# First-batch context first, two weight transfers instead of four, and a layer 1 that opens on the rounded half of its input

## The reference, cut to what matters

```python
# x: (8, 256, 256)   ctx: (8, 120, 256)   w1, w2: (1024, 256)   h1, h2: (1024, 1024)   w3: (256, 1024)
n = layernorm(x)
x = x + (gelu_tanh(n @ ctx.T) * (n @ ctx.T)) @ ctx       # per batch, the "attention" part
n = layernorm(x)
h = silu(n @ w1.T * s1) * (n @ w2.T * s2)                # layer 1
h = gelu(h @ h1.T * sh1)                                 # the two square layers
h = gelu(h @ h2.T * sh2)
x = x + h @ w3.T * s3                                    # layer 4
```

## Time and profile before

| | us |
|---|---|
| median of 3 runs | 334.35 |
| lowest, highest | 331.96, 334.93 |
| the profiled execution, its own time | 334.1 |
| its span in the profile | 332.3 |
| PE busy | 324.5 (98%) |
| DVE busy | 264.6 (80%) |
| ACT busy | 218.1 (66%) |
| POOL busy | 47.3 (14%) |

### The profile page before, as it was taken

The page is one execution under the profiler, slowest core; times in us unless marked ns, Lnnn a source line. Parts: engine busy times, 40 slices in busy tenths (PEclk is TensorE's granted clock), DMA queues, the critical chain, the costliest instruction groups (busy, mean ns, idle before and its releaser), DMA issues.

```text
span 332.3 us, 4771 instructions
## 1 busy us (share of the span) xinstructions
PE 324.5 (98%) x1643; PEld 274.4 (83%) x1643; DVE 264.6 (80%) x492; ACT 218.1 (66%) x367; POOL 47.3 (14%) x86
## 2 busy tenths in 40 slices
PE   7999999999999999999999999999999999999994
PEld 4699888888878888888998888888887888888994
DVE  3577888796996999998579666398899798987594
ACT  2355838648596886778914564977679687785840
POOL 6247020201100022112130003000100000110000
PEclk9999999999999999999999999999999999999999
DMA  7769999949657762735306033345575863443003
GB/s 227 257 208 292 207 225 368 407 172 306 192 176 250 284 240 90 228 129 155 100 0 231 24 126 126 128 127 189 189 225 197 278 249 130 126 131 123 0 32 104
DMA packets 23213, 60.22 MB, mean 181 GB/s; under 512 B 1680, under 2 KB 7184, under 8 KB 20880
## 3 DMA queue, kind: packets, MB, share of 16 engines
q0 software_dynamic: 13728, 37.75, 38.0%
q1 hardware_dynamic: 9168, 21.60, 19.0%
q10 hardware_dynamic: 288, 0.51, 0.5%
HBM read 49.36 MB, written 6.29 MB: 167 GB/s over the span
## 4 chain that ended last, share of the span: by engine, by line
PE 95%; DVE 1%; DMA 1%; POOL 1%; issue 0%; ACT 0%; DVEq 0%
PE P L1290 61%; PE P L1242 18%; PE P L1319 9%; PE P L1214 2%; PE P L1198 2%; PE P L1206 2%; DMA xs<-in_x 1%; POOL rs L434 1%; PE P L1391 1%; PE P L1384 1%; PE P L1398 0%; PE P L1329 0%; DVE xn L819 0%; POOL rs L432 0%; DVE xs L831 0%
## 5 line engine op out<-in xcount | busy, mean ns | idle before, releaser
L1290 PE MATMUL P<-TR,WR 128*128 128x512 f32 x896 | 205.5, 390 | 0.0
L1290 PEld LDWEIGHTS P<-TR,WR 128*128 128x128 f32 x896 | 167.7, 188 | 35.4 <-DVE H L915 0.8
L591 ACT ACTIVATE TR<-H 128x512 fp32r<-128x512 f32 x112 | 68.1, 626 | 29.1 <-DVE H L894 26.4
L899 DVE TENSOR_TENSOR TR<-H,TR 128x512 fp32r<-128x512 f32 x112 | 73.8, 686 | 7.6 <-ACT TR L591 5.9
L1242 PE MATMUL P<-X,W 128*128 128x512 f32 (+1 forms) x320 | 62.7, 351 | 0.1
L1242 PEld LDWEIGHTS P<-X,W 128*128 128x128 f32 x320 | 51.7, 189 | 8.1 <-DVE X L836 0.5
L894 DVE TENSOR_TENSOR H<-H 128x512 f32<-128x512 f32 x64 | 42.0, 684 | 0.0
L872 DVE SCALAR_TENSOR_TENSOR H<-P,sc,SLY 128x512 f32<-128x512 f32 (+1 forms) x40 | 25.2, 639 | 19.1 <-ACT SLY L581 10.0
L581 ACT ACTIVATE SLY<-P,sc 128x512 f32<-128x512 f32 (+1 forms) x40 | 23.7, 601 | 18.6 <-PE P L1242 18.4
L605 ACT ACTIVATE H<-P 128x512 f32<-128x512 f32 x48 | 27.8, 593 | 11.6 <-PE P L1290 11.6
L625 ACT ACTIVATE H<-H,sc 128x512 f32<-128x512 f32 x40 | 27.4, 713 | 10.7 <-DVE H L915 10.7
(11 more groups left out here) (72 smaller groups left out, 197.9 us busy)
## 6 DMA issues: line engine op xcount, KB each, us to landing
WR<-blocks_h POOLq DMA_DIRECT2D x16, 1024.0 KB, 5.1
WR<-in_h POOLq DMA_DIRECT2D x12, 1024.0 KB, 5.2
H<-in_h POOLq DMA_DIRECT2D x8, 512.0 KB, 12.0
blocks_h<-H SPq DMA_DIRECT2D x4, 1024.0 KB, 6.6
SLY<-in_h SPq DMA_DIRECT2D x8, 512.0 KB, 4.5
SLY<-in_w SPq DMA_DIRECT2D x6, 512.0 KB, 4.6
W<-in_w POOLq DMA_DIRECT2D x4, 512.0 KB, 7.8
WR<-in_w POOLq DMA_DIRECT2D x2, 1024.0 KB, 5.1
```

The lines of the kernel that those rows point to most:

```text
L591: eng.activation(TR[:, f % RING, 0, :], operand(c, L, s, kk), ACT.Copy).then_inc(s_hi, 1)
L899: eng.tensor_tensor(TR[:, f % RING, 1, :], operand(c, L, s, kk), TR[:, f % RING, 0, :].bitcast(f32), ALU.subtract).then_inc(s_lo, 1)
L1290: out_ = eng.matmul(bank(c, L, s, m)[:, :], WR[r % WRING][:, at:at + 128], TR[:, f % RING, h, :], start=(s in FRESH[L] and kk == 0 and h = ...
```

## The change

In the beginning of the program:

- The context arrays lie in memory with the batch ahead of the feature half, so that one batch's part is one transfer. ACT no longer issues them. SP issues, in this order: the two halves of `x` of batch 0, context of batch 0 (two transfers, with semaphores `e_cf` and `e_ct`), `x` of batch 1, context of batch 1 (two transfers), the scales.
- POOL issues `W12` in two transfers (w1, then w2) instead of four, after waiting for `s_tab`, which ACT signals when its first table load is done.
- On PE `score(1)` no longer stands ahead of layer 1. The first half of layer 1 waits for `s_X0` and runs the rounded parts of groups 0 and 1 (two matmuls each), waits for `s_X1`, runs their other parts, then `score(1)`, then groups 2 to 15. `weigh(1)` follows group 5 instead of group 3.
- `score(2)` moves from between the two halves to behind group 1 of the second half.
- The filler counts become 16, 3, 3, 2, 16, 3 instead of 16, 2, 2, 1, 14, 2.

```diff
-SPIN = (16, 2, 2, 1, 14, 2)
+SPIN = (16, 3, 3, 2, 16, 3)
...
# SP
             for j in range(2):
                 eng.dma_start(xs[:, j, :], x_v[0, :, j, :]).then_inc(s_x0[j], 16)
+            eng.dma_start(cf[:, 0, 0, :, :], ctx_feat[:, 0, 0, :, :]).then_inc(e_cf, 16)
+            eng.dma_start(ct[:, 0, 0, :], ctx_tok[:, 0, :]).then_inc(e_ct, 16)
             load_x(1)
+            eng.dma_start(cf[:, 0, 1, :, :], ctx_feat[:, 0, 1, :, :]).then_inc(s_cf[0], 16)
+            eng.dma_start(ct[:, 0, 1, :], ctx_tok[:, 1, :]).then_inc(s_ct[0], 16)
             eng.dma_start(sc[:, :], cols).then_inc(s_sc, 16)
-            for i in range(4):
+            for i in range(2):
                 eng.wait_ge(s_w12[i], 16)
...
# POOL
             def load_w12(i):
-                eng.dma_start(W12[:, i % 2, i // 2, :], w12[i % 2][:, i // 2, :]).then_inc(s_w12[i], 16)
+                eng.dma_start(W12[:, i, :, :], w12[i]).then_inc(s_w12[i], 16)
...
-            for i in range(4):
+            eng.wait_ge(s_tab, 1)
+            for i in range(2):
                 load_w12(i)
...
# ACT
             table(ACT.Gelu_apprx_tanh)
-            eng.dma_start(cf[:, 0, :, :, :], ctx_feat[:, 0, :, :, :]).then_inc(s_cf[0], 16)
-            eng.dma_start(ct[:, 0, :, :], ctx_tok[:, 0:2, :]).then_inc(s_ct[0], 16)
...
# PE
-            def group(t, i, p=1):
+            def group(t, i, p=1, parts=(0, 1)):
...
-                    for h in range(2):
+                    for h in parts:
...
             def attend(t, i):
+                if (t, i) == (0, 1):
+                    score(2)
...
             def layer1(t):
                 if t == 0:
+                    eng.wait_ge(s_X0, 1)
+                    for i in range(2):
+                        eng.wait_ge(s_w12[i], 16)
+                        group(0, i, 0, (0,))
                     eng.wait_ge(s_X1, 1)
-                    for i in range(16):
-                        if i < 2:
-                            eng.wait_ge(s_w12[i], 16)
-                            eng.wait_ge(s_w12[2 + i], 16)
+                    for i in range(2):
+                        group(0, i, 0, (1,)).then_inc(s_mm1, 1)
+                    score(1)
+                    for i in range(2, 16):
                         if i >= 6:
                             consumed(eng, 0, i - 6, 0)
                         group(0, i, 0).then_inc(s_mm1, 1)
-                        if i == 3:
+                        if i == 5:
                             weigh(1)
...
-                    score(2)
...
# score_half waits for e_cf and weigh_half for e_ct; the index order of cf follows the new layout
...
             turn_half(1, 1)
-            score(1)
             for c in range(NC):
                 layer1(2 * c)
```

More of the change, by code:

```diff
@@ L120, in xattn_ffn @@
         s_ct = [sem(f"s_ct{t}") for t in range(NT)]
+        e_cf, e_ct = sem("e_cf"), sem("e_ct")
         s_sc, s_s3 = sem("s_sc"), sem("s_s3")
-        s_w12 = [sem(f"s_w12{i}") for i in range(4)]
+        s_w12 = [sem(f"s_w12{i}") for i in range(2)]
         s_raw = [sem(f"s_raw{i}") for i in range(4)]
@@ L398, in _ @@
                     eng.dma_start(gx[:, :, :], x_v[b]).then_inc(g_in, 16)
-                    eng.dma_start(gcf[:, :, :], ctx_feat[:, b // 2, :, b % 2, :]).then_inc(g_in, 16)
+                    eng.dma_start(gcf[:, :, :], ctx_feat[:, b // 2, b % 2, :, :]).then_inc(g_in, 16)
                     eng.dma_start(gct[:, :], ctx_tok[0:S, b, :]).then_inc(g_in, 16)
@@ L1205, in score @@
                 for c in range(2):
-                    out_ = eng.matmul(side(b)[0:S, 0:TB], cf[:, (b // 2) % 2, c, b % 2, :], xt[:, b % 2, c, :],
+                    out_ = eng.matmul(side(b)[0:S, 0:TB], cf[:, (b // 2) % 2, b % 2, c, :], xt[:, b % 2, c, :],
                                       start=(c == 0), stop=(c == 1))
@@ L1239, in group @@
                 for k in range(2):
-                    w = W12[:, v, k, m * 128:(m + 1) * 128]
-                    for h in range(2):
-                        out_ = eng.matmul(bank1(t, i, p)[:, at], w, X[:, t % 2, h, k, at],
+                    for h in parts:
+                        out_ = eng.matmul(bank1(t, i, p)[:, at], W12[:, v, k, m * 128:(m + 1) * 128], X[:, t % 2, h, k, at],
                                           start=(k == 0 and h == 0), stop=(k == 1 and h == 1))
@@ L1387, in score_half @@
             def score_half(j):
-                eng.wait_ge(s_cf[0], 16)
+                eng.wait_ge(e_cf, 16)
                 half_done(eng, j, e_xt, 1, s_xt)
                 for c in range(2):
-                    out_ = eng.matmul(piece(j)[0:S, 0:128], cf[:, 0, c, 0, :], xt[:, 0, c, j * 128:(j + 1) * 128],
+                    out_ = eng.matmul(piece(j)[0:S, 0:128], cf[:, 0, 0, c, :], xt[:, 0, c, j * 128:(j + 1) * 128],
                                       start=(c == 0), stop=(c == 1))
@@ L1395, in weigh_half @@
             def weigh_half(j):
-                eng.wait_ge(s_ct[0], 16)
+                eng.wait_ge(e_ct, 16)
                 half_done(eng, j, e_h, 1, s_h)
@@ L1516 @@
         "ctx_tok": np.pad(c.transpose(1, 0, 2), ((0, 128 - S), (0, 0), (0, 0))),
-        "ctx_feat": c.reshape(NT, 2, S, 2, 128).transpose(4, 0, 3, 1, 2),
+        "ctx_feat": c.reshape(NT, 2, S, 2, 128).transpose(4, 0, 1, 3, 2),
         "w1": by_input(L0_ffn_w1_w), "w2": by_input(L0_ffn_w2_w),
```

## The result

| | before | after |
|---|---|---|
| median of 20 runs, us | 333.45 | 335.14 |
| lowest, highest | 331.96, 334.98 | 334.66, 339.1 |
| the profiled execution, its own time | 334.1 | 335.05 |
| its span | 332.3 | 333.3 |

The ratio after to before is 1.0066, with a 95% interval of 1.0045 to 1.0086: 0.7% slower, 2.2 us by the ratio, 1.7 us between the medians. The prediction said 336.7 with a range of 334.2 to 338.3, and that the direction is up by less than 1%.

A forecast was written before the change was run, and what follows sets the result against it. PE was taken to bound the kernel (95% of the chain), with score(1)'s chain through DVE pacing layer 1's first half. Profiled 334.1 + 0.1 (start) + 1.62 (score(1)) + 0.86 (score(2)) = 336.7 us, range 334.2 to 338.3.

The forecast's parts named there:

- score(1) and its chain: First half of layer 1: later score(1) delays gelu, table load, silu, both, and so the end, by 1.62 us.
- a wait of PE at turn(1,1): Sign in the first half of layer 1: PE newly waits about 1 us for xn at batch 1's transpose.
- a silu(0) before 18.5: Sign in layer 1's first half: silu(0) expected at 19.4 us; before 18.5 would break the largest term, 1.62.
- rival A: First half of layer 1: DVE catches up, so only PE's own +0.38 us counts; 335.4 us, chance 0.14.
- score(2), 0.86 predicted: Second half of layer 1: score(2) leaves PE's wait between halves for time where PE is busy, costing 0.86 us.
- The start: Before layer 1: filler cost of +0.2 us less a 0.1 gain from the transfers, net +0.1 us.
- Rival B: First transposes to 10.6 us: low clock ends sooner through filler and earlier x; 334.3 to 335.2, chance 0.13.
- The gain of x: Start: x of batch 0 has fewer transfers beside it, gaining 0 to 0.4 us; 0.1 was taken.
- POOL is done between 3.4 and 4.6: Start: POOL finishes issuing W12 then, its first rstd work starting about 4.5 as before; worst 0.1 us.
- The fillers' +0.2: Start, PE: extra fillers at the low clock, 0.22 us each, make the add 0.15 to 0.2 us late.
- C: Idle PE ahead of turn(1,1) and the second half lets the clock fall, costing 2.2 us: 338.9, chance 0.13.
- D: Layer 1: PE gets through 0.5 us sooner, the 1.62 not behind score(1), B on top: 332.1 or below, chance 0.07.

The follow-up runs named there:

- g1: Kernel after with weigh(1) behind group 3 instead of group 5, score(1) still behind groups 0 and 1: 335.18 us, ratio to before 1.0065.
- g2: Kernel after with score(1) back ahead of layer 1 and weigh(1) behind group 3: 333.45 us, ratio to before 1.0017.
- f1: Kernel before with the new PE order alone, transfers and fillers as before: 335.26 us, ratio to before 1.0072.
- e2: Kernel after with score(1) back ahead of layer 1, weigh(1) still behind group 5: 334.15 us, ratio to before 1.0030.
- e1: Kernel after with score(2) back between the two halves of layer 1: 334.29 us, ratio to before 1.0024.
- h1: Kernel before with 20 instead of 16 fillers in the first block: 333.09 us, ratio to before 0.9988.
- f4: e3 with POOL issuing w2 only behind the two first rstd steps of batch 0: 332.35 us, ratio to before 0.9976.
- f3: Kernel before with the new filler counts alone: 332.94 us, ratio to before 0.9998.
- e4: Kernel after with the filler counts of before: 335.41 us, ratio to before 1.0066.
- e3: Kernel after with all of PE's order of before, keeping the new transfers and fillers: 332.69 us, ratio to before 0.9977; its profiled run took 335.52.

## Why the prediction was right, and where a size was off

**score(1) and its chain, 1.62 predicted: right.** g1 against g2 gives 1.73 by the medians and 1.67 by the profiles, and the ruler 1.69. The order of events is the forecast one: gelu, table load, silu, both, all shifted by what score(1) was shifted; a wait of PE at turn(1,1) (1 us said, 0.80 seen), 0.2 at group 11 (0.3 said). The prediction also said that a silu(0) before 18.5 would break this term, and silu(0) came at 17.87. That sign was set on absolute times: the rounded input was ready 1.46 us sooner than before, and from it to silu(0) it took 3.97 us for 2.29, 1.68 more, so the term stands. PE's own view, rival A with 0.38, is refuted by f1 and by g2, though its 335.4 lay nearer to the measured time than the forecast's 336.7. What the prediction did not see is that the move of weigh(1) has a price of its own, 0.54 us (g2 against e2), which shows only once score(1) is early.

**score(2), 0.86 predicted: right.** e1 gives 0.85 in the median and in the window (9.06 for 9.91 us), and PE idles 1.18 us ahead of the second half where 1.2 was said.

**The start, +0.1 predicted: wrong in size, -1.5 against the profiled execution of before.** The sum stood on an execution that belongs to the upper of that kernel's two groups, with the slow clock until about 10 us. The kernel after's profile has the fast clock from about 7 us, and reaches the rounded input at 13.90 instead of 15.36, 1.46 sooner. Rival B had this: 1.5 us, and a time of 335.2, where 335.05 was profiled and 335.14 is the median; it had score of half 0 at 7.2, the add at 9.15, and they came at 7.09 and 9.18. What B gave as the reason, filler and an earlier x, is not shown: f1 and h1, with the old transfers, have the fast clock at the first transpose too, so the early rise looks like what the kernel before does in its lower group. So the mechanism that I gave 0.13 came true on top of the forecast's two terms, and 336.7 is what the forecast makes of the late clock. That the number fell into the range owes something to luck: the two terms of the PE order were right, the start was off by about 1.6 us, and the range was wide enough to hold that. The hint was in the rows at hand: 331.96 beside 334.35 and 334.93. With the groups compared like with like (before's lower one around 332.6), the terms give 332.6 + 1.62 + 0.86 = 335.1.

Within that step, smaller ones. The gain of x was bounded by 0.4 and was 0.81 at its arrival (2.95 for 3.76), but only 0.38 of it passed through POOL, which issued W12 until 4.10; that is the cover that "POOL is done between 3.4 and 4.6" named and took as harmless. f4 took it away and won 0.43 us at the first transpose, of which its times show nothing. POOL began to issue at 2.84 us, 0.6 behind the end of ACT's dummy, where the prediction had it begin at once. The fillers' +0.2 was priced at the low level; at the high level they lie in waits, and f3 and e4 find no cost. W12 came at 12.49 for 12.41, in time. The late landing of x of batch 1, named as a possible loss, is the rare case that e3's profile caught. In the chances, a tenth of the forecast's 0.53 is 0.05, which makes 0.75 for "same" and 0.18 for slower, not 0.76 and 0.17.

The Trainium skill's rule on keeping TensorE busy (TensorE: Matmul & The Clock Gate, "Why this matters for your kernels"), by which more filler would be a gain and not a cost, is not borne out by a run here and not refuted: neither f3 nor e4 finds a gain or a cost, and h1 leans its way without settling it. The Trainium skill's statement that the monitor runs free of the kernel (same page, "What's actually happening") is compatible with the two groups of runs; what sets the share of each stays open.

**Rivals C and D** did not come: the matmuls of layer 1 behind the new idle times of 0.80 and 1.18 us run at the full pace (eight in 1.20 us at 23.99 and in 1.22 at 27.31), and nothing made up for score(1). What C feared does exist: in e3's profile the clock fell behind an idle time of 2.09 us, from 11.5 to 14.7.

## What to carry to other kernels

Idle time of the bounding engine is free room only for work on which nobody waits: starting matmuls 0.5 us sooner moved a score behind them whose gelu, table load and silu pace the whole stretch, and cost 1.7 us. Moving work out of a wait that stays costs its full duration, here 0.86 us. Before a sum is built on one profiled execution, look where that execution lies among the runs; where they fall into two groups, price each step in both, and set signs as distances from an event that the change doesn't move, not as absolute times.

## What was not expected of the hardware

The granted clock does not show the first slow stretch. In the kernel before, this window reads 1.00 while the matmuls in it run at half their later pace:

```profile
5.96:10.40 4.44, 4.43 (x18) 3.55 (x19) 1.90 (x7) 1.32 (x4) 1.35 (x3) 1.00 1.10 366
```

Only the durations tell (three fillers in 0.85 or in 0.49 us). The later fall in e3 does show, as 0.50. The first 128 KB transfer of x, issued at 0.73, was there after 2.1 to 2.3 us in the ten profiles with the new transfers, and after 2.6 to 3.0 in the four with the old ones, where ACT issues a context transfer 0.13 us later and POOL its first weights at 1.73; which of the two slows it wasn't tested. x of batch 1, issued at the same moment of the same transfer order, took from 3.2 us (the kernel after) to 6.4 us (e3).
